# Convolution attention: the attend product as three fp32r products of high and low parts, and queries and keys from one projection

## The reference, cut to what matters

```python
xf = x.reshape(B, Ch, N)                                  # 8, 128, 1024
q = jnp.einsum('oc,bcn->bon', Wq, xf) + bq[None, :, None] # 64 channels
k = jnp.einsum('oc,bcn->bon', Wk, xf) + bk[None, :, None] # 64 channels
v = jnp.einsum('oc,bcn->bon', Wv, xf) + bv[None, :, None] # 128 channels
scores = jnp.einsum('bcm,bcn->bmn', q, k)
attn = jax.nn.softmax(scores, axis=1)
out = jnp.einsum('bcn,bmn->bcm', v, attn)
return gamma * out.reshape(B, Ch, H, W) + x
```

## Time and profile before

| what | value |
|---|---|
| median of 3 runs (lowest to highest) | 1437.9 us (1436.93 to 1439.31) |
| the profiled execution: its own time, its span | 1436.42 us, 1434.7 us |
| busy share of the span: PE, PEld, DVE, ACT, POOL | 83%, 72%, 64%, 39%, 41% |
| first projection starts; `finish` of the last image starts; whitening starts | 7.07 us; 224.08 us; 227.5 us |

### The profile page before, as it was taken

One profiled execution on the slowest core, in us unless ns is written; L12 is line 12 of the kernel. 1 busy time (PEld: TensorE's weight loads), 2 busy tenths in 40 slices (PEclk: granted clock), 3 DMA queues, 4 the chain that ended last, 5 costly groups with the idle time before them and its releaser, 6 DMA issues. The chain is left out here.

```text
span 1434.7 us, 31184 instructions
## 1 busy us (share of the span) xinstructions
PE 1192.1 (83%) x11614; PEld 1030.4 (72%) x11614; DVE 919.6 (64%) x2231; ACT 561.0 (39%) x1293; POOL 590.4 (41%) x651
## 2 busy tenths in 40 slices
PE   7999998888482999999996663858489999999960
PEld 4555557677472999999994543635489999999960
DVE  4777775578661754466642876575638777788862
ACT  3444442146360655555554531533233332332310
POOL 5000002000336767757304772067300774577675
PEclk9999999899655999999997885669559999999985
DMA  8600000000402334434324110011002333334343
GB/s 321 283 0 1 0 1 9 1 1 1 141 21 69 115 119 129 123 113 119 100 64 165 51 45 2 1 47 53 26 30 67 119 112 103 104 109 117 106 133 104
DMA packets 87095, 115.66 MB, mean 81 GB/s; under 512 B 18371, under 2 KB 71142, under 8 KB 86694
## 3 DMA queue, kind: packets, MB, share of 16 engines
q1 hardware_dynamic: 65990, 62.92, 14.0%
q0 software_dynamic: 20960, 50.76, 10.9%
HBM read 53.19 MB, written 60.42 MB: 79 GB/s over the span
## 5 line engine op out<-in xcount | busy, mean ns | idle before, releaser
L1419 POOL DMA_INDIRECT sorted_rows<-s_normed,s_places x128 | 135.7, 1060 | 179.3 <-DVE s_places L1365 138.7
L1496 POOL DMA_INDIRECT gx_fetch<-sorted_results,g_places x128 | 132.6, 1036 | 129.4 <-DMA sorted_results<-gx_yq 66.5
L1496 POOL DMA_INDIRECT sx_fetch<-sorted_results,s_places x128 | 137.4, 1073 | 84.7 <-issue 32.8
L1579 PE MATMUL g_bank<-weights,gx_hT 128*128 x1360 | 165.7, 275 | 0.0
L1419 POOL DMA_INDIRECT sorted_rows<-g_normed,g_places x128 | 131.6, 1028 | 67.7 <-issue 36.3
L1579 PEld LDWEIGHTS g_bank<-weights,gx_hT 128*128 128x128 f32 x1360 | 158.4, 192 | 0.5 <-issue 0.5
L1542 PE MATMUL s_bank<-sx_xT_high,sx_w_now 128*128 128x256 f32 (+1 forms) x510 | 151.8, 298 | 1.1 <-DVE sx_hT L1654 0.6
L1544 PE MATMUL s_bank<-sx_xT_high,sx_w_now 128*128 128x256 f32 (+1 forms) x510 | 144.1, 283 | 0.0
L1543 PE MATMUL s_bank<-sx_xT_low,sx_w_now 128*128 128x256 f32 (+1 forms) x510 | 143.9, 282 | 0.0
L1607 ACT ACTIVATE gx_hT<-g_bank,gx_b_now 128x256 f32<-128x256 f32 x340 | 133.0, 482 | 3.0 <-PE g_bank L1579 3.0
L1579 PE MATMUL s_bank<-weights,sx_hT 128*128 (+1 forms) x1020 | 129.7, 276 | 2.9 <-DVE sx_yq L1665 1.4
(11 more groups left out here) (423 smaller groups left out, 2729.5 us busy)
## 6 DMA issues: line engine op xcount, KB each, us to landing
sorted_rows<-zeros POOLq DMA_DIRECT2D x29, 512.0 KB, 15.5
gx_xq<-sorted_rows SPq DMA_DIRECT2D x85, 128.0 KB, 2.0
sorted_results<-gx_yq SPq DMA_DIRECT2D x85, 128.0 KB, 1.9
sx_xq<-sorted_rows SPq DMA_DIRECT2D x85, 128.0 KB, 2.1
sorted_results<-sx_yq SPq DMA_DIRECT2D x85, 128.0 KB, 2.0
feats<-in_x SPq DMA_DIRECT2D x8, 512.0 KB, 7.0
out<-tokens SPq DMA_DIRECT2D x16, 256.0 KB, 4.0
s_raw<-in_silu_up SPq DMA_DIRECT2D x1, 2736.0 KB, 9.9
```

The source lines that it names most:

```text
L1419: pool.indirect_dma_start(out=sorted_rows[g], out_offset=bass.IndirectOffsetOnAxis(ap=places[:, at, r:r + 1], axis=0), in_=normed[:, at, : ...
L1496: pool.indirect_dma_start(out=fetch[n % 2][:, i, r, :], out_offset=None, in_=self.sorted_results[g], in_offset=bass.IndirectOffsetOnAxis(a ...
L1579: done = pe.matmul(down[u % 2][:, P * k:P * k + C], hT[u % 2][0:width, i, P * k:P * k + P], self.w_down[0:width, bass.ds(e, 1), i, :].rear ...
```

## The change

The attend product becomes three fp32r products. `probs` of a chunk is split in `p_high`, rounded to fp32r, and `p_low`, the rest; the scaled values are split in `vs_high` and `vs_low`. TensorE adds `vs_high` times `p_high`, `vs_high` times `p_low` and `vs_low` times `p_high`. The parts come from three engines: ScalarE rounds columns 0 to 767 of `p_high`, VectorE columns 768 to 1023; GpSimd subtracts to get the 1024 columns of `p_low`; ScalarE writes `vs_high` with the inverted sum as scale, and VectorE writes `vs_low` in one instruction (v times the inverted sum, less `vs_high`). `scale_values` goes. `lag` becomes 3, and `probs`, `p_high` and `p_low` have three buffers each (`probs` had four). GpSimd's 34 zero fills are spread over the chunks, behind each `low_of`, and no longer wait for the last image.

From image 2 on, queries and keys come from one projection with the weights [q, k], 64 output channels each, so that an image has four items (two of both, two of values), at n = 1, 3, 5, 6 on TensorE and one chunk later on VectorE and ScalarE. Rounded part and rest then lie in `q_high` and `q_low`, queries on the lower and keys on the upper 64 partitions. SP moves the keys into `k` with two DMAs, waits for both, and then copies the queries to the upper halves with two more. Images 0 and 1 are projected as before. The host's packed array has 644 columns in place of 515.

The diff, cut to its core (declarations of tiles and semaphores, and the counting of items, are left out):

```diff
-    lag = 2
+    lag, kept, by_act = 3, 3, 768
...
+            low, high = slice(0, CQ), slice(CQ, P)
+            for b in range(APART, B):
+                sp.wait_ge(qk_ready, taken_until(b, 2))
+                sp.dma_start(k[b % 2][low, :].bitcast(F32), q_high[b % 2][high, :].bitcast(F32)).then_inc(moved, 16)
+                sp.dma_start(k[b % 2][high, :].bitcast(F32), q_low[b % 2][high, :].bitcast(F32)).then_inc(moved, 16)
+                sp.wait_ge(moved, 32 * (b + 1 - APART))
+                sp.dma_start(q_high[b % 2][high, :].bitcast(F32), q_high[b % 2][low, :].bitcast(F32)).then_inc(doubled, 16)
+                sp.dma_start(q_low[b % 2][high, :].bitcast(F32), q_low[b % 2][low, :].bitcast(F32)).then_inc(doubled, 16)
...
         @block.gpsimd
+            def low_of(s):
+                pool.wait_ge(high_by_act, s + 1)
+                pool.wait_ge(high_by_dve, s + 1)
+                if s >= kept:
+                    pool.wait_ge(av_done, s + 1 - kept)
+                pool.tensor_tensor(p_low[s % kept][:, :], probs[s % kept][:, :], p_high[s % kept][:, :].bitcast(F32),
+                                   ALU.subtract).then_inc(low_ready, 1)
...
-            pool.wait_ge(x_loaded[B - 1], 16)
...
+            for s in range(TT):
+                low_of(s)
+                for rows, at in fills[len(fills) * s // TT:len(fills) * (s + 1) // TT]:
...
             def scores(b, n):
...
+                    if b >= APART:
+                        pe.wait_ge(doubled, 32 * (b + 1 - APART))
...
             def attend(b, n):
                 pe.wait_ge(vs_ready, s + 1)
+                pe.wait_ge(low_ready, s + 1)
...
-                    done = pe.matmul(out[:, HALF * h:HALF * h + HALF], vs[s % 4][:, :],
-                                     probs[s % 4][:, HALF * h:HALF * h + HALF], start=(n == 0), stop=(n == NT - 1))
+                    high, low = p_high[s % kept][:, at], p_low[s % kept][:, at]
+                    pe.matmul(out[:, at], vs_high[s % 4][:, :], high, start=(n == 0), stop=False)
+                    pe.matmul(out[:, at], vs_high[s % 4][:, :], low, start=False, stop=False)
+                    done = pe.matmul(out[:, at], vs_low[s % 4][:, :], high, start=False, stop=(n == NT - 1))
...
         @block.vector
+            def invert_sum(s):
+                dve.wait_ge(exp_done, s + 1)
...
+                dve.reciprocal(rz[s % 4][:, :], zsum[s % 4][:, :]).then_inc(rz_ready, 1)
+            def take_high(s):
+                if s >= kept:
+                    dve.wait_ge(av_done, s + 1 - kept)
+                dve.tensor_copy(p_high[s % kept][:, by_act:], probs[s % kept][:, by_act:]).then_inc(high_by_dve, 1)
+            def scale_values_low(s):
+                dve.wait_ge(vs_high_ready, s + 1)
...
+                dve.scalar_tensor_tensor(out=vs_low[s % 4][:, :], in0=v[s // NT % 2][:, s % NT, :],
+                                         scalar=rz[s % 4][:, 0:1], in1=vs_high[s % 4][:, :].bitcast(F32),
+                                         op0=ALU.mult, op1=ALU.subtract).then_inc(vs_ready, 1)
...
                 row_max(s)
                 if s >= 1:
-                    scale_values(s - 1)
+                    invert_sum(s - 1)
+                    take_high(s - 1)
+                if s >= 2:
+                    scale_values_low(s - 2)
...
         @block.scalar
+            def take_high(s):
...
+                act.activation(p_high[s % kept][:, 0:by_act], probs[s % kept][:, 0:by_act], ACT.Copy
+                               ).then_inc(high_by_act, 1)
+            def scale_values_high(s):
+                act.wait_ge(rz_ready, s + 1)
...
+                act.activation(vs_high[s % 4][:, :], v[s // NT % 2][:, s % NT, :], ACT.Copy, scale=rz[s % 4][:, 0:1]
+                               ).then_inc(vs_high_ready, 1)
...
                 exponent(s)
+                take_high(s)
+                if s >= 1:
+                    scale_values_high(s - 1)
```

More of the change, by code:

```diff
@@ L130, in conv_attention @@
     x = ins["x"].rearrange("b c h w -> b c (h w)")
-    lag = 2
+    lag, kept, by_act = 3, 3, 768
     with ExitStack() as ctx:
         t = ClearedTools(nc, ctx)
[L134 to L137, removed]
+        packed = t.sbuf("conv_packed", [P, 5 * C + 4])
+        wT = [packed[:, P * i:P * i + P] for i in range(4)]
+        bv = packed[:, 4 * C:5 * C]
+        bq, bk, bqk, gamma = (packed[:, 5 * C + i:5 * C + i + 1] for i in range(4))
         q_high = [t.sbuf(f"q_high{i}", [P, N], F32R) for i in range(2)]
@@ L141, in conv_attention @@
         v = [t.sbuf(f"v{i}", [P, NT, C]) for i in range(2)]
-        probs = [t.sbuf(f"probs{i}", [P, N]) for i in range(4)]
-        vs = [t.sbuf(f"vs{i}", [P, C]) for i in range(4)]
+        probs = [t.sbuf(f"probs{i}", [P, N]) for i in range(kept)]
+        p_high = [t.sbuf(f"p_high{i}", [P, N], F32R) for i in range(kept)]
+        p_low = [t.sbuf(f"p_low{i}", [P, N], F32R) for i in range(kept)]
+        vs_high = [t.sbuf(f"vs_high{i}", [P, C], F32R) for i in range(4)]
+        vs_low = [t.sbuf(f"vs_low{i}", [P, C], F32R) for i in range(4)]
         nmax = [t.sbuf(f"nmax{i}", [P, 1]) for i in range(4)]
@@ L168, in conv_attention, with items_of, pairs_of, given_until @@
         cleared = t.sem("cleared")
+        APART = 2
+        PLACES = {6: (1, 2, 3, 4, 5, 6), 4: (1, 3, 5, 6)}
+        def items_of(b):
+            return 6 if b < APART else 4
+        def pairs_of(b):
+            return items_of(b) - 2
+        def given_until(b, items):
+            return sum(items_of(i) for i in range(b)) + items
+        def taken_until(b, items):
+            return sum(pairs_of(i) for i in range(b)) + items
         block = ctx.enter_context(nc.Block())
@@ L204, in project @@
                 else:
-                    pe.wait_ge(qk_ready, b * 4 + item - 1)
+                    pe.wait_ge(qk_ready, taken_until(b, item - 1))
                 bank = proj[item % 2]
-                if item < 4:
-                    w = wT[item // 2]
+                if item < pairs_of(b):
+                    w = wT[item // 2 if b < APART else 3]
                     pe.matmul(bank[:, :], w[:, :], feats[:, b, HALF * (item % 2):HALF * (item % 2) + HALF],
@@ L262, in take_low @@
             def take_low(b, item):
-                dve.wait_ge(qk_high, b * 4 + item + 1)
+                dve.wait_ge(qk_high, taken_until(b, item + 1))
                 at = slice(HALF * (item % 2), HALF * (item % 2) + HALF)
-                if item < 2:
+                if b >= APART:
+                    high, low, rows, bias = q_high[b % 2], q_low[b % 2], slice(0, P), bqk
+                elif item < 2:
                     high, low, rows, bias = q_high[b % 2], q_low[b % 2], slice(0, P), bq
@@ L313, in _ @@
                 if s >= 1:
-                    scale_values(s - 1)
[L315 to L319, removed]
+                    invert_sum(s - 1)
+                    take_high(s - 1)
+                if s >= 2:
+                    scale_values_low(s - 2)
+                if b + 1 < B and n - 1 in PLACES[items_of(b + 1)]:
+                    take_item(b + 1, PLACES[items_of(b + 1)].index(n - 1))
+                if lag < n <= lag + 2 and b > 0:
+                    measure(b - 1, n - lag - 1)
+            invert_sum(TT - 1)
+            take_high(TT - 1)
+            scale_values_low(TT - 2)
+            scale_values_low(TT - 1)
             finish(B - 1)
```

64 lines of the change are left out of this document (38 added, 26 removed).

## The result

The kernel after takes 1439.03 us (median of 20 runs, 1433.7 to 1442.71), the kernel before 1433.88 (20 runs): ratio 1.0037, 95% interval 1.0024 to 1.0051. It is slower by 0.37%, or 5.2 us by the medians, where I forecast 18 us less. The execution from which the forecast was counted, 1436.42, lay 2.5 above the median of the kernel before.

What follows compares the result with a forecast made beforehand. VectorE and GpSimd together were to set the pace after the change, TensorE just under it. -23.2 + 2.3 + 0.2 + 2 + 1 = -17.7 against 1436.4 gave 1418.7, forecast as 1419 us; range 1407 to 1436.

Steps and rivals of the forecast that it cites:

- the DMA term: Moving queries and keys on SP's queue: stalls of 0 to 2.1 us for each of six images, 2 us taken in all.
- The cover: Time the moves may take, from VectorE's last rest at n = 4 to the next image's first scores: 7.9 us.
- The length: Time for two successive DMA steps of two 256 KB moves: 4.6 to 10 us, with 8.0 the middle.
- My own signs for a wrong forecast: Scaling of 2 us in many chunks, growing PSUM side jobs, first scores waiting over 1 us for DMA, or falling clock.
- The fills: 34 zero fills behind GpSimd's subtractions: covered there, but slowing VectorE's copies in expert stages by 0 to 8.4 us, 1 taken.
- VectorE's pair of 0.55: Per chunk, VectorE's 256-column copy for p_high and its vs_low instruction, both locking out GpSimd: 0.55 us together.
- my sum is -23.2 + 2.3: Two forecast terms: the stage gets 23.2 us shorter, and the longer chain at its end costs 2.3 more.
- The alternation: VectorE and GpSimd take turns at their shared port: 2.16 + 0.55 = 2.71 us for a chunk, setting the pace.
- the lower bound: Most of a VectorE instruction could hide in GpSimd's start, so the alternation could cost as little as 2.2 us a chunk.
- the scaling kept the port: Rival that vs_low loses the port to GpSimd's subtraction: such a chunk 1.4 us more, 1441 to 1510 us; chance 0.10.
- One SBUF input beside PSUM: Rival that GpSimd also blocks VectorE's items' rests, values and finish: 70 us more, 1489 us; chance 0.05.
- the last rival, the gain given back: Hand-overs of 0.2 a chunk (about 11 us) and slow DMA steps (11 more): 1436 to 1441 us; chance 0.09.

Runs made afterwards that it cites:

- Run 3: The changed kernel with the second item projected at n = 2 instead of n = 3, so the DMA moves start a chunk earlier; ratio to before 0.9929.
- run 9: The changed kernel with the second item a chunk earlier and the zero fills issued on SP's queue after both DMA steps; ratio to before 0.9867.
- run 10: Like run 9, but ScalarE makes 896 instead of 768 of the 1024 columns of p_high; ratio to before 0.9857.
- run 5: The changed kernel with GpSimd subtracting only 512 of 1024 columns, leaving out the other half's low part; ratio to before 1.0000.
- 2: The changed kernel with the zero fills moved out of the chunks in which keys and queries travel; ratio to before 0.9987.
- 4: The changed kernel with both the fills moved out of the moves' way and the second item one chunk earlier; ratio to before 0.9934.
- 6: The changed kernel with the second item one chunk earlier and GpSimd subtracting only 512 columns; ratio to before 0.9872.
- 7: The changed kernel with the second item one chunk earlier and all fills within the first 56 chunks; ratio to before 0.9934.
- run 8: The kernel before with only the joint query and key projection and its DMA moves, attend product still fp32; ratio to before 0.9986.
- 1: The changed kernel with only the three-part attend product, queries and keys projected apart for every image, no moves; ratio to before 0.9953.

## Why the prediction was wrong

**The step that failed is the DMA term**, "So 0 to 2.1 for each of six images, 0 to 13; a stall stops TensorE and all behind it. I take 2 in all.". The term failed in its cover, in its length, and in what a stall does.
- The cover: I counted 7.9 by VectorE's chunks. TensorE comes to the scores 7.0 after the first move: it is busy for 7.00 of the 7 us from 107 on, so it waits for nobody in this stretch, VectorE included.
- The length: 8.5 with no fill beside the second step, 10.6 with one. I had 8.0, with 10 as the upper end, and priced no transfer of the fills beside the moves, though the next paragraph has the fills spread over the same chunks. The two transfers of the first step land 2.9 and 3.8 after their issue (medians), and the second is issued 0.5 later: 4.3 for the first step.
- What a stall does: I took it at its length. The half clock behind the three long ones adds some 5.8 us, and the other engines run dry: VectorE and ScalarE have no work from 117 to 117.84, so nothing that was ahead stays ahead.

Run 3 prices the term, with what the moved item does besides: 16.5 us where I took 2 and had 13 as the upper end. My own signs for a wrong forecast, a stall of over 1 us at an image's first scores and a falling clock, both came.

The Trainium skill ("SBUF — State Buffer", section "Can I just issue two DMAs to hit both halves?") says that two transfers on the two halves of the partitions run one behind the other. The first step, which writes both halves, agrees as far as it goes: its transfers land at 2.9 and 4.3, so 1.4 apart, though issued 0.5 apart. No run issues one of them alone. I had let the two of a step run side by side.

**The fills** were the second mis-sized term: 1 taken, 5.7 measured (run 9 against 3, with the 0.5 of the stall left in 3), inside the bound of 8.4. I named VectorE's pair of 0.55 as their cover. A fill takes 0.55 itself, and a turn gets 0.2 longer (2.91 against 2.70). The last one cost a whole 1.0 at the barrier, which I had not looked at.

**The rest held.** Without the moves' stall and without the fills on GpSimd my sum is -23.2 + 2.3 = -20.9; run 9, whose second item comes a chunk earlier than in the kernel that I forecast, has 190.45 against 210.90, which is -20.45. Here too two errors cancel: up to the end of the last row maximum run 9 is 24.6 shorter (I had 23.2), and from there to `finish` it takes 8.3, so 4.1 more than before, where I had 2.3 more.
- TensorE's products start 0.23 apart, and an image takes TensorE at most 22.2 (run 10), forecast 22.3.
- The alternation is there, at 2.68 a turn against 2.71, but by two errors that cancel. The subtraction takes 2.40, not 2.16: the line through 128 and 684 columns does not hold for it, and already 512 columns take 1.295 (run 5) where the line gives 1.19. `vs_low` lies beside the start of the next subtraction and adds nothing, as the lower bound had it. So a turn is 2.40 + 0.28. The Trainium skill ("GPSIMD Engine Reference", section 3.1) has 4497 ns for 2048 columns of a two-input add. The estimate of 2.26 that I drew from it was nearer than the one from my rows, and still too low.
- An image set by the alternation takes 22.5 (run 9); the forecast was 22.7. That it is so near is in part luck: by the starts of the subtractions it has six turns of 2.7, one of 2.8 and one of 3.6, where I had six and two of 3.2.
- Of the rivals, the scaling kept the port but for one chunk: in the kernel after `vs_low` has a median of 340 ns against 345; the longest, in the last chunk, took 2.74 us. One SBUF input beside PSUM is not blocked: the items' rests take 742 ns against 745. Of the last rival, the gain given back, the DMA half came, with more than its worst price (16.5 against 13); its hand-overs of 0.2 a chunk did not. That its 1436 to 1441 holds the 1439 measured is in part luck.

**What stays open.** By the profiled executions the kernel after is 2.4 us longer (1438.83 against 1436.42): 1.3 by the end of the stage and the rest behind it. The medians differ by 5.2, since the profiled execution of the kernel before lay 2.5 above its median and that of the kernel after 0.2 below. In runs 2, 3, 4, 6, 7 and 8 the time by the ratio gains 4 to 8 us less than the stage, in 1, 5, 9 and 10 it follows it within 1.5; the intervals are some 2 to 4 us to each side. The part behind the stage, which moves by 8.5 us over the twelve profiles, is large enough to hold that; what moves it, one profile for each kernel cannot show.

## What to carry to other kernels

A wait that is newly laid behind a DMA is hidden only for as long as the work in front of it takes, and the same change may make that work faster: count the cover at the pace of after and at the engine that waits, and start the transfer as early as its data is there. Look at which other transfers are issued beside it, since a fill that nobody waits for lengthened one that the whole stage waits for. When a change has two halves, time each alone; here, by the stage, both gained alone and the pair lost.

## What the runs showed that I had not expected

- The clock behind a stall: after three idle stretches of TensorE of 3.5 to 3.6 us it was at 0.50 for 8 to 13 matmuls, while after the stalls of 1.5 to 1.6 matmuls kept 0.23. In one case it was down before the first matmul (89.28), in another the first four matmuls from 117.84 still ran at full pace and the next eight did not.
- The same two moves of 256 KB took 2 us longer with one fill of 512 KB beside the second step: 5.7 to landing for the later one, against 3.5 to 3.6 in the images of the same kernel without one, and a median of 3.5 in run 9. Not every long step has a fill beside it: in run 8 the first steps from 108.79 and 184.13 took 5.3 and 5.0 in place of 4.15, long after the last fill, and why is open.
- A DMA issue of 0.55 us on GpSimd's queue lengthened a turn of 2.70 by 0.2 although VectorE works in the same gap.
